# One of the two shared parts that run in units among the expert blocks is run whole, behind the fifth part and ahead of the first block

## The reference

```python
shared_out = silu(x @ shared_gate_w.T) * (x @ shared_up_w.T) @ shared_down_w.T   # x: (4096, 256), inner size 256
routing_weights = softmax(x @ router_weight.T)                                    # 32 experts
top_idx = top_k(routing_weights + e_score_bias, 6)
# weights of the 6 chosen ones, normed to a sum of 1 -> combine (4096, 32)
hmid = silu(gate) * up                     # of each expert, inner size 128
y = einsum('tei,ehi->teh', hmid, down_proj)
out = einsum('teh,te->th', y, combine) + shared_out
# x = x + gb * out, with x the result of the attention and gb a gate for each batch
```

## Time and profile before

| | us |
|---|---|
| median of 3 timed runs | 779.85 (778.77 to 779.91) |
| the profiled execution | 775.63 |
| its span, first to last instruction | 773.8 |
| PE busy | 714.7 (92%) |
| DVE busy | 482.6 (62%) |
| POOL busy | 410.9 (53%) |
| ACT busy | 391.9 (51%) |

### The profile page before, as it was taken

How to read it: one execution, slowest core, us unless ns; L and a number is a source line. 1 busy time by engine, 2 the same in 40 slices (tenths; PEclk the granted TensorE clock), 3 DMA queues, 4 the chain that set the end, 5 groups by cost and what they waited for, 6 DMA issues and landing times.

```text
span 773.8 us, 13345 instructions
## 1 busy us (share of the span) xinstructions
PE 714.7 (92%) x4326; PEld 586.9 (76%) x4326; DVE 482.6 (62%) x1258; ACT 391.9 (51%) x927; POOL 410.9 (53%) x420
## 2 busy tenths in 40 slices
PE   4988989998997998849999899999999999999994
PEld 3566668676676565549999899999999999998451
DVE  3887889799889628415555344444444545445998
ACT  5484755854661552126566455555565666654000
POOL 0000000667777777777777776774666666666100
PEclk9999999999999999969999999999999999999998
DMA  9510010243353998367777876775766666569995
GB/s 322 162 66 0 1 55 0 103 155 109 124 182 119 383 415 318 128 233 216 256 249 232 275 239 208 229 235 151 230 200 189 188 206 196 184 230 391 399 411 194
DMA packets 82620, 158.30 MB, mean 205 GB/s; under 512 B 14446, under 2 KB 55667, under 8 KB 82296
## 3 DMA queue, kind: packets, MB, share of 16 engines
q1 hardware_dynamic: 58344, 96.60, 37.9%
q0 software_dynamic: 19968, 56.67, 20.1%
q10 hardware_dynamic: 4240, 4.19, 1.6%
HBM read 88.02 MB, written 73.57 MB: 209 GB/s over the span
## 4 chain that ended last, share of the span: by engine, by line
PE 65%; DVE 11%; POOL 11%; issue 5%; ACT 4%; DMA 2%; SPq 1%; DVEq 0%; ACTq 0%; POOLq 0%
PE ps_wide L1330 17%; PE ps_wide L1345 12%; POOL expert_rows L560 11%; PE ps_kv L1330 8%; PE ps_narrow L1318 6%; PE ps_wide L1093 5%; PE ps_wide L1086 3%; DVE arena L1652 3%; PE ps_kv L1093 2%; PE ps_kv L1354 2%; PE ps_narrow L1045 1%; PE ps_kv L1423 1%; DVE arena L1912 1%; PE ps_narrow L1423 1%; DMA arena<-expert_rows 1%
## 5 line engine op out<-in xcount | busy, mean ns | idle before, releaser
L560 POOL DMA_INDIRECT expert_rows<-arena,slot_i x192 | 193.0, 1005 | 200.4 <-DVE arena L1646 136.8
L664 POOL DMA_INDIRECT expert_outs<-arena,meta x224 | 217.7, 972 | 108.3 <-DVE arena L1863 65.6
L898 ACT COPY arena<-arena 128x512 f32 x224 | 127.4, 616 | 153.3 <-PE ps_narrow L1318 146.1
L1863 DVE TENSOR_SCALAR arena<-ps_wide,meta 128x256 f32<-128x256 f32 x224 | 98.1, 480 | 127.2 <-PE ps_wide L1345 126.8
L1330 PEld LDWEIGHTS ps_wide<-arena 128*128 128x128 f32 x1200 | 146.5, 193 | 3.9 <-issue 0.2
L1330 PE MATMUL ps_wide<-arena 128*128 128x128 f32 x1200 | 147.2, 276 | 0.0
L1345 PE MATMUL ps_wide<-arena 128*128 x448 | 115.3, 380 | 0.9 <-DVE arena L1839 0.5
L1345 PEld LDWEIGHTS ps_wide<-arena 128*128 128x128 f32 x448 | 76.5, 190 | 7.3 <-issue 1.5
L1318 PE MATMUL ps_narrow<-cst,arena 128*128 128x128 f32 x448 | 68.8, 276 | 14.2 <-DMA arena<-expert_rows 14.2
L881 ACT COPY arena<-ps_narrow 128x512 f32<-128x512 f32 x112 | 64.7, 578 | 19.6 <-PE ps_narrow L1318 19.6
L1330 PEld LDWEIGHTS ps_kv<-arena 128*128 128x128 f32 x592 | 71.7, 192 | 1.9
(11 more groups left out here) (241 smaller groups left out, 1017.8 us busy)
## 6 DMA issues: line engine op xcount, KB each, us to landing
arena<-expert_rows SPq DMA_DIRECT2D x224, 160.0 KB, 2.9
arena<-expert_outs SPq DMA_DIRECT2D x48, 512.0 KB, 12.4
arena<-w_experts SPq DMA_DIRECT2D x32, 384.0 KB, 15.8
expert_rows<-pad_row SPq DMA_DIRECT2D x33, 160.0 KB, 5.1
expert_outs<-arena,meta POOLq DMA_INDIRECT x224, 3.4
out<-x ACTq DMA_DIRECT2D x7, 512.0 KB, 11.6
x<-x SPq DMA_DIRECT2D x3, 1024.0 KB, 11.2
h_cols<-arena SPq DMA_DIRECT2D x6, 512.0 KB, 3.9
```

The lines of the kernel that those rows point to most:

```text
L560: nc.gpsimd.indirect_dma_start(rows, bass.IndirectOffsetOnAxis(ap=slots_i[b % 2][:, t, k:k + 1], axis=0), hrows[b % 2][:, t, :], None, bou ...
L664: nc.gpsimd.indirect_dma_start(outs, bass.IndirectOffsetOnAxis(ap=meta_i[:, j % METAS, 1:2], axis=0), yb[j % OUTS], None, bounds_check=las ...
L898: last = nc.scalar.copy(wgu[:, j % 4:j % 4 + 1, :], wall[:, bass.ds(expert[j], 1), 0:DOWN])
L1863: v.tensor_scalar(yb[j % OUTS], ps_wide[:, 1, p % 2, j % DUO * D:(j % DUO + 1) * D], meta[:, j % METAS, 0:1], None, ALU.mult).then_inc(s_y ...
```

## The change

Part 5 joins the whole parts, part 6 becomes the one of the tail, and part 7 alone stays in units, so that there are two units, from pair 40 on, and their load stands behind group 10. Part 5's h2 is loaded into the first half of `h2t` once part 2 has been read from it, and its product is held in `tail_in[0]`, which part 4 read from. On PE `shared_gate(5)` stands between up 4 and down 4, and `shared_up(5)` and `shared_down(5)` behind down 4, all ahead of `turn_blocks(0)`. ACT's silus run to part 5 before the blocks (`range(2, BEFORE)`, L874), and POOL's three waits that name `BEFORE` now name down 4, up 5 and down 5. Pair 2's gate and up wait for `shared_add(5)` instead of 4 (L1396).

```diff
--- before.py
+++ after.py
@@ -67,9 +67,9 @@
 PARTS = NT // PART
 
 ORDER = [0, 1, PARTS - 2, PARTS - 1] + list(range(2, PARTS - 2))
-BEFORE = 5
-LAST, AMONG = [BEFORE], [BEFORE + 1, BEFORE + 2]
-TAIL = [0, 1, 2, 3, LAST[0], 4] + AMONG
+BEFORE = 6
+LAST, AMONG = [BEFORE], [BEFORE + 1]
+TAIL = [0, 1, 2, 3, LAST[0], 4, 5] + AMONG
 UNIT = PART // 2
 UNITS = [(i, n) for i in AMONG for n in range(PART // UNIT)]
 assert sorted(TAIL) == list(range(PARTS))
@@ -267,10 +267,10 @@
         unit_mid = take(C, UNIT * P, overlay=tail_at + (OUTS - BUF) * D)
         in_two = [rcst[:, 0:HALF], in_rope]
         shared_in = ([late[2], late[1]] + [h2t[:, :, hf * HALF:(hf + 1) * HALF] for hf in range(HALVES)]
-                     + [tail_in[0], in_ranks, in_ranks, None])
+                     + [tail_in[0], h2t[:, :, 0:HALF], in_ranks, None])
         shared_cols = [[i[:, c, :] for c in range(C)] if i is not None else in_two for i in shared_in]
         mid = ([late[0], late[2]] + [take(C, HALF, overlay=h2_at + i * C * HALF) for i in range(2)]
-               + [tail_in[1], take(C, HALF, overlay=h2_at)])
+               + [tail_in[1], tail_in[0], take(C, HALF, overlay=h2_at)])
         rope_rows = take(2, TILES, HW, overlay=rope_at)
         moments = take(TPH, 6, overlay=rope_at + 2 * TILES * HW)
         mean_var = take(TPH, 2, overlay=rope_at + 2 * TILES * HW + TPH * 6)
@@ -451,6 +451,9 @@
             for e in range(E - LATE, E):
                 sp.dma_start(wall[:, e], w_experts[:, e]).then_inc(s_wall, 16)
 
+            sp.wait_ge(s_su, 3)
+            load_h2(5)
+
             def write_padding(e):
 
                 first = nc.values_load(pad_at[0:1, e:e + 1], engines=(SP,), min_val=0, max_val=E * REGION - P,
@@ -1386,7 +1389,10 @@
             shared_gate(4)
             shared_down(3)
             shared_up(4)
+            shared_gate(5)
             shared_down(4)
+            shared_up(5)
+            shared_down(5)
             turn_blocks(0)
             pe.wait_ge(s_wall, 16 * E)
             pe.wait_ge(s_wgu, 1)
@@ -1883,6 +1889,8 @@
             shared_add(3)
             shared_mid(4)
             shared_add(4)
+            shared_mid(5)
+            shared_add(5)
             keep_meta(0)
             keep_meta(1)
             for p in range(DUOS):
```

## The result

| | before | after |
|---|---|---|
| median, us | 779.88 (778.77 to 780.91, 4 runs) | 765.93 (764.94 to 766.71, 4 runs) |
| ratio | | 0.9824, interval 0.9809 to 0.9839 |
| profiled execution, us | 775.63 | 766.71 |
| its span, us | 773.8 | 764.8 |

The medians lie 13.95 us apart (forecast 12.8, to 767.0), the two profiled spans only 9.0. Both numbers need explaining, and the second is the one that the trace can explain. Part of the distance between them is which executions were profiled: that of the kernel before took 4.2 us less than its median, that of the changed kernel 0.8 us more than its own.

The account below looks back on a forecast made before the run. PE was taken as the bound, except that POOL's scatters decide when the blocks begin. Block 112 moving from 535.14 to 522.3 gave 12.8 us: 779.85 - 12.8 = 767.0, 80% range 764.8 to 770.8.

Parts of the forecast that it names:

- Units removed, 10.4 us: Before block 112, two of four units leave PE's path: 2 x 3 steps of 1.73 us, 10.4 us gained.
- The table stall, 2.26 us: PE's stall at 427 to 430 goes as the units' loads move behind group 10: 2.26 us gained, bounds 0 to 2.26.
- Part 5 in the gap, 0 us: Ahead of the first block, 10.3 us of new PE work fits PE's idle time and costs 0, with 0.66 us spare.
- POOL's waits and stream: POOL's changed waits are past by 5 us or more; scatters stay 1.28 us apart, the last at 515.4.
- Block 112, 0 to 1.5 us: At block 112's transposes PE, ready at 522.5 or 521.1, waits 0 to 1.5 us for its load; 522.3 taken.
- rival A: POOL's stream binds by more: waits or DMAs slip 1 to 4 us, block 112 later, gain 9 to 12; chance 0.13.
- The clock: Part 5 in the gap may keep PE at 2.4 GHz, limit 521.1, or the clock falls again from 337 to 342, 522.5.
- Nothing behind block 112: Behind block 112 nothing has a time of its own: blocks stay at 3.09 us a pair, the tail keeps one whole part.
- The step from the profile to the median: The timed median, 779.85, is 4.2 us above the profiled execution; nothing in it scales, so the full 12.8 us comes off.
- B: The gap doesn't hold part 5: PE reaches block 0 late by 1 to 3 us, gain 10 to 12; chance 0.07.
- C: The unit loads stall again: 2.26 us return at pairs 40 to 44, gain 10.4, 769.4; chance 0.07.
- D: Part 5's load lands late and holds down 4 and every block; at 340 some 4.5 us slower, 784.4; chance 0.02.

Follow-up runs that it names:

- 18 scatters and the stall: Changed kernel with 18 instead of 16 scatters ahead of put 0 and the units' load and table wait back behind group 6: 766.74 us, ratio 0.984.
- the stall put back alone: Changed kernel with the units' load and its table wait back behind group 6, 16 scatters ahead: 766.49 us, ratio 0.9825.
- more work in the gap: Changed kernel with 8 unused matmul records between up 5 and down 5: 764.33 us; the same with 18 scatters ahead: 761.3 us.
- chip 5: Chip on which the kernel before took 853.16 us and the unedited changed kernel 862.22 us, ratio 1.0084; three edits of the changed kernel also ran there.

## Why the prediction was right, and where it was not

*Units removed, 10.4 us.* Right: with two units and the stall gone PE reached block 112 13.4 us earlier, and the stall's share of it is below.

*The table stall, 2.26 us.* Mechanism right, size too small. The idle times of the earlier trace rows leave out what a stall costs around itself. The pairs' starts in the profile of the kernel before (with one unit step, 1.73 us, between the first two) and the next:

```profile
419.82 1.95 PE L1330 MATMUL ps_wide<-arena 128*128 128x128 f32 x16
...
424.97 1.95 PE L1330 MATMUL ps_kv<-arena 128*128 128x128 f32 x16
...
431.02 1.95 PE L1330 MATMUL ps_wide<-arena 128*128 128x128 f32 x16
```

From pair start to pair start these took 5.15 and 6.05 us, where 3.09 + 1.73 and 3.09 were due: 0.33 + 2.96 = 3.3 us. 10.4 + 3.3 - 0.2 (this execution ran 0.2 us late already at 318.75) = 13.5, against 13.4 measured. With the clock down it costs more still. By the same count it was 4.8 us in the profile with 18 scatters and the stall (4.6 by the medians), 5.7 with the stall put back alone, and in the second profile of the kernel before 8.57 - 3.09 = 5.5 for the pair of the stall and 6.91 - 3.09 - 1.73 = 2.1 for the next, 7.6 in all.

*Part 5 in the gap, 0 us.* Right to the step: down 5 at 334.05 was forecast for 333.7, the first transposes at 338.05 for 337.86 or later. (The 3.43 and 3.45 us of the prediction are distances between starts in that timeline; the earlier trace rows shows lengths, 3.60 and 3.72.) The spare was underrated. The first pair of experts waits for four blocks, not for block 0 alone, so 3.43 us more fitted too. PE's two waits over 1 us here (1.39 and 1.90) stand in the kernel before too, in the same places (1.38 and 1.44), and the prediction's times contain them, though its sign "a wait of PE over 1 us before pair 54", taken by the letter, does not leave them out.

*POOL's waits and stream.* Right: last scatter at 515.51, forecast 515.4.

*Block 112, 0 to 1.5 us.* The step that was mis-sized in the trace. Its own landing (by 522.09, forecast 521.9) was right, but a pair needs two blocks. Block 113 was issued behind it and was found 1.9 us later, and the clock fell with the wait: 4.4 us in all. The forecast of 522.3, set beside PE's readiness at 521.7, left 0.6. That is rival A in its effect, by another path than the slip of POOL's stream that it named. The size varies: in the second profile of the changed kernel it was 1.9 us, with the clock at 1.00.

*The clock.* It was 1.00 from 332 to 336, where the kernel before had 0.50, and fell between 337 and 342 (0.86), the case that the prediction left open. The two runs with more work in the gap show the other one: clock 1.00, first pair 1.95 us. The rule of the Trainium skill (TensorE: Matmul & The Clock Gate, section What's actually happening), that recent activity releases the throttle, agrees with 0.85 against 1.00 in the two windows. It does not settle what part 5 alone does: with the same PE work ahead, the clock fell in five profiles and stayed at 1.00 in a sixth.

*Nothing behind block 112.* Right: from the start of pair 56 to the end of the span it is 234.2 to 234.3 us in both profiles of the kernel before and in the eight of the changed kernel and its variants outside chip 5.

*The step from the profile to the median.* "I know of nothing in it that scales" was wrong. The profiled execution of before was 4.2 us under its median. The second profile and the granted clocks of 23 executions show why such a distance exists: the waits ahead of the first pairs and in the table stall differ between executions, and so does how far the clock falls in them. The change takes the stall away, which cost 3.3 us in one profile and 7.6 in the other. It does not take away the low clock of the first pairs, which five of six profiles without extra work still have. In medians 13.95 us were gained, in the two profiles 9.0; of the 4.95 between, 4.2 lie in the profile of before and 0.8 in that of the changed kernel. No profile of an execution at the median exists, so how its 4.2 us are spread over the two places is not shown.

*The number.* The forecast of 767.0 came within 1.1 us of 765.93 by two errors that cancel: a loss at block 112 that was too small by about 4 us, and some 5 us between profiles and medians that it did not have. For the profiled execution itself the same sum said 762.8, and it took 766.71. That the median came out so close is luck; that it fell is not.

*Rivals B, C and D* did not happen in the result's profile: no PE wait over 0.5 us between 342 and 522, and part 5's load, issued at 301.74, landed in 8.2 us, 12 us ahead of its use. On chip 5 the gap was gone, which B had only as 1 to 3 us.

## What to carry to other kernels

Work moved into an idle stretch is free as long as the stretch is set by another engine, and what it gains on the bound engine can then run into that other engine's next deadline, as here: compute the second limit too, for the last piece that the step needs (here the second block of the pair). Shifting two scatters ahead was worth another 3 to 4 us behind the change. In the kernel before PE reached block 112 without a wait (535.14), so by the trace little was to be gained there; that was not run. And a stall on PE is to be read from pair start to pair start, and over several executions where the clock can fall in it.

## What the runs showed of the hardware

The same table stall, 1.45 us of waiting for its block in one execution and 2.89 in another, cost PE 3.3 us in the one and 7.6 in the other. In the one the granted clock stayed at 1.00; in the other it was 0.77 from 425 to 440, with 3.62 us for 16 matmuls instead of 1.95. Unused matmuls ahead of a wait went with a clock of 1.00 in both profiles that had them and lost no time (764.33 against 765.93 and 765.13 us); one profile of six without them had 1.00 as well. GpSimd started one indirect DMA every 1.28 us, for 127 in a row, whatever VectorE did beside it. And one chip ran the same kernels 9 to 13% slower (853 and 862 against 780 and 766 us), with pauses of PE up to 7.6 us that no engine or DMA in the profile accounts for; on it the change made the kernel slower by 0.5 to 1.1% instead of faster by 1.8%.
